# Cross-attention with routed experts: the next pair's keys and values loaded a step and a half ahead, the first normalisation in slot 2 of its own step

## The reference

```python
# 16 heads of 16; the mask pads queries' keys, and the scores are causal
x = x + tanh(g_xattn) * (softmax(mask(heads(layernorm(x)) @ heads(ctx).T / 4)) @ heads(ctx) @ W.T + b)
z = layernorm(x)
shared = swiglu(z @ w_in.T) @ w_out.T
# 2 groups of 4 experts: argmax of the group, softmax inside it, the top 2 of it by weight w_se
routed = sum over e of (swiglu(z @ w1.T) * w_se[:, e]) @ w2[e].T
x = x + tanh(g_ffn) * (shared + routed)
```

## Time and profile before

| | us |
|---|---|
| median of 3 runs (1431.3 to 1433.97) | 1433.58 |
| the profiled execution | 1430.63 |
| its span, first to last instruction | 1428.8 |
| PE busy in the span | 1201.9 (84%) |
| DVE busy | 865.6 (61%) |
| ACT busy | 502.2 (35%) |
| POOL busy | 552.0 (39%) |

### The profile page before, as it was taken

The page is one execution under the profiler, slowest core; times in us unless marked ns, Lnnn a source line. Parts: engine busy times, 40 slices in busy tenths (PEclk is TensorE's granted clock), DMA queues, the critical chain, the costliest instruction groups (busy, mean ns, idle before and its releaser), DMA issues.

```text
span 1428.8 us, 22394 instructions
## 1 busy us (share of the span) xinstructions
PE 1201.9 (84%) x7387; PEld 953.1 (67%) x7387; DVE 865.6 (61%) x1968; ACT 502.2 (35%) x780; POOL 552.0 (39%) x658
## 2 busy tenths in 40 slices
PE   0577988888888888888888898626999999999997
PEld 0245766666666666666766666525888888888886
DVE  4435667466466567566466567773666666666665
ACT  3334434443444444444443443222222222222221
POOL 1112222422422422422522514354555656555543
PEclk9989999999999899999899899867999999999999
DMA  5466435445435335435435321343222222222210
GB/s 161 85 112 114 93 81 100 85 83 95 88 74 100 84 80 101 85 80 100 86 80 98 73 47 46 75 118 83 63 71 65 65 68 73 65 64 66 69 42 9
DMA packets 108263, 115.30 MB, mean 81 GB/s; under 512 B 36942, under 2 KB 88433, under 8 KB 108148
## 3 DMA queue, kind: packets, MB, share of 16 engines
q1 hardware_dynamic: 96376, 85.41, 29.1%
q0 software_dynamic: 11776, 28.46, 6.7%
HBM read 50.44 MB, written 28.64 MB: 55 GB/s over the span
## 4 chain that ended last, share of the span: by engine, by line
PE 57%; DVE 10%; DMA 8%; POOL 8%; issue 7%; SPq 5%; ACT 4%; POOLq 0%; ACTq 0%; DVEq 0%
PE ps L681 14%; PE ps L699 10%; DMA af<-in_ctxT 7%; PE ps L702 5%; PE ps L635 5%; PE ps L618 5%; POOL tab_dram L1375 3%; PE ps L541 3%; PE ps L526 3%; PE ps L550 3%; POOL gl L1358 2%; SPq L421 2%; PE ps L502 2%; PE ps L497 2%; PE ps L594 1%
## 5 line engine op out<-in xcount | busy, mean ns | idle before, releaser
L699 PE MATMUL ps<-w2a,gh 128*128 x608 | 218.7, 399 | 0.0
L702 PE MATMUL ps<-w2a,gl 128*128 x608 | 170.6, 281 | 0.0
L759 ACT ACTIVATE Pt<-ps,pbias 77x1024 f32<-77x1024 f32 x128 | 141.5, 1106 | 73.6 <-PE ps L528 73.1
L1358 POOL TENSOR_TENSOR gl<-gf,gh 128x512 fp32r<-128x512 f32 x64 | 82.6, 1290 | 148.1 <-ACT gh L801 148.1
L1303 POOL TENSOR_SCALAR ve<-mv 128x2 f32<-128x2 f32 x64 | 15.6, 244 | 317.0 <-DVE mv L882 316.4
L1411 POOL DMA_INDIRECT out<-ot,Pt x76 | 78.4, 1032 | 153.2 <-DVE ot L1232 149.7
L699 PEld LDWEIGHTS ps<-w2a,gh 128*128 128x128 f32 x608 | 114.3, 188 | 25.2
L681 PE MATMUL ps<-z2h,w1h 128*128 128x512 f32 x304 | 122.0, 401 | 7.4 <-DVE z2l L886 7.4
L618 PE MATMUL ps<-x2h,winh 128*128 128x512 f32 x256 | 124.3, 486 | 2.4 <-DVE gf L1157 1.5
L1093 DVE TENSOR_REDUCE mneg<-ps 128x8 f32<-128x616 f32 x128 | 101.6, 795 | 35.8 <-PE ps L502 35.7
L681 PE MATMUL ps<-z2l,w1h 128*128 128x512 f32 x304 | 121.1, 398 | 0.0
(11 more groups left out here) (205 smaller groups left out, 2858.7 us busy)
## 6 DMA issues: line engine op xcount, KB each, us to landing
w2a<-w2a SPq DMA_DIRECT2D x96, 256.0 KB, 5.8
af<-in_x SPq DMA_DIRECT2D x32, 256.0 KB, 4.1
x<-in_x SPq DMA_DIRECT2D x32, 256.0 KB, 7.0
y_dram<-xn SPq DMA_DIRECT2D x32, 256.0 KB, 3.5
y_dram<-res SPq DMA_DIRECT2D x32, 256.0 KB, 2.6
w2a<-w2a SPq DMA_DIRECT2D x96, 77.0 KB, 2.8
Pt<-in_w2T SPq DMA_DIRECT2D x16, 256.0 KB, 3.0
af<-in_ctxT SPq DMA_DIRECT2D x16, 154.0 KB, 6.8
```

What stands on the lines that cost most here:

```text
L699: e.matmul(o, gh2[:, c % 2, fc, t * P:(t + 1) * P], w2v[:, bass.ds(val, 1), fc, :, :].rearrange("p o h d -> p (o h) d"), start=fc == 0, st ...
L702: m = e.matmul(o[:, 0, :], gl2[:, c % 2, fc, t * P:(t + 1) * P], w2v[:, bass.ds(val, 1), fc, 0, :].rearrange("p o d -> p (o d)"), start=Fa ...
L759: e.activation(Pt[0:K, 4 * k:4 * k + 4, :].rearrange("k (n j) t -> k n (j t)", n=2), bank_of["sc", b, k][0:K, :, :], ACT.Exp, bias=pbias[: ...
L1358: e.tensor_tensor(gl[:, fc - 1, :], gf[:, n % 2, :], gh[:, fc - 1, :].bitcast(F), ALU.subtract).then_inc(s["gl"], 1)
```

## The change

Three things move in `phase_one`; no stage is added, taken away or changed inside.

- kv moves from slot 0 to slot 3 of the even step, and load_kv of the next pair from the end of the odd step to slot 8 of the even step, so that it stands 19 slots before the kv that reads it.
- norm of batch i moves from slot 11 of step i-1 to slot 2 of step i. The norm of batch 0, which stood ahead of the steps, is in slot 2 of step 0.
- load_x of batch i+2 moves from slot 0 of step i to slot 3, behind kv, since it has to follow the norm that frees the buffer.

```diff
     order += [("load_x", 0, 0), ("load_x", 1, 0), ("load_kv", 0, 0), ("own", 0, 0), ("moments", 0, 0),
-              ("norm", 0, 0), ("masks", 0, 0)]
+              ("masks", 0, 0)]
...
-        put(i, ((7, "xT", 0), (10, "queries", 0)))
-        put(i + 1, ((8, "moments", 0), (11, "norm", 0)))
+        put(i, ((2, "norm", 0), (7, "xT", 0), (10, "queries", 0)))
+        put(i + 1, ((8, "moments", 0),))
         if i % 2 == 0 and i < NB:
-            slots[0].append(("kv", i // 2, 0))
+            slots[3].append(("kv", i // 2, 0))
+            if i + 2 < NB:
+                slots[8].append(("load_kv", i // 2 + 1, 0))
...
-            if slot == 0 and i + 2 < NB:
+            if slot == 3 and i + 2 < NB:
                 order.append(("load_x", i + 2, 0))
...
-        if i % 2 == 1 and i < NB - 1:
-            order.append(("load_kv", i // 2 + 1, 0))
```

## The result

| | before | after |
|---|---|---|
| median of 4 runs each, us | 1432.44 | 1341.51 (1338.39 to 1343.35) |
| profiled execution | 1430.63 | 1338.39 |
| its span | 1428.8 | 1336.6 |
| mean granted clock | 0.929 | 0.953 |

The ratio is 0.9373, 95% interval 0.9335 to 0.941: faster, by 91 us of the medians and 92.2 us of the two profiled spans.

The account below looks back on a forecast made before the run. TensorE was the engine to fill, stalled behind the key load. Gains 4.9 + 3.4 + 14.5 + 6 x 2.7 + 6 x 4.0 = 63 us off 1430.63 gave 1367.6, forecast as 1369; main range 1355 to 1385, 8-in-10 range 1336 to 1404.

Parts of the forecast that it names:

- The load's stall: TensorE's waits at L550 behind the key load: 59.2 us of gaps, plus up to 33 us lost at the lower clock.
- The start and the pairs without routing: Before the routed pairs: 4.9 us from the weights' splits, 3.4 in the first pair, 14.5 in the other two.
- What is late next in B: POOL's fixed chain from scatters to gl sets the limit; TensorE waits longer than 3.34 us at L635; gain about 3.2 us.
- B: Six pairs of steps whose eight routing scatters run on POOL in the first step; forecast gain 4.0 us each (2.6 to 5.5).
- The norm: First normalisation moved to slot 2: 4.9 us at the start, 0.88 us at gl in each B, nothing in A.
- A: Six pairs of steps with routing arithmetic on DVE in both steps; forecast gain 2.7 us each (1.0 to 4.4).
- The two gaps: TensorE waits left in A: 1.2 us at O, about 1.75 at the max matmul; 1.7 us of low clock charged for both.
- Rival 1: Nothing takes the place of TensorE's stalls: 64 + 33 + 4.9 = 102 us gained, so 1331 us; chance 0.15 (1331 to 1355).
- Rivals 3 and 4: maxT's DMA late in SyncE's queue: either no gain left, 1433 us, chance 0.05, or slower, 1459 us, chance 0.04.
- I take 0: Loss from maxT's DMA L424 landing later behind the moved loads: taken as 0 us, at most 39 us in 15 pairs.
- The other signs: Phase one's mean clock above 0.91, ACT's and POOL's waits for the load gone, weights' split on ACT 4.9 us earlier.

Follow-up runs that it names:

- the filled stall: The kernel before, with 30 unused small matmuls in front of O in each even step from the fourth on: 1410.82 us, ratio 0.9865.
- part 1 alone: The kernel before with only kv moved to slot 3 and load_kv to slot 8, norm and load_x as before: 1363.75 us, ratio 0.9507.
- part 2 alone: The kernel before with only the norm moved to slot 2 of its own step and load_x to slot 3: 1418.13 us, ratio 0.9892.
- the fastest version: The changed kernel with three routing pieces per two slots instead of four, and the second normalisation's root moved behind gl: 1274.61 us, ratio 0.8919.

## Why the prediction was right or wrong, step by step

- **The load's stall goes, and it cost twice.** Right. L550's 59.2 us are 4.9, and the filled stall shows the second cost by itself: 19 us.
- **The start and the pairs without routing.** Right: 9.3 against 8.3 (4.8 with part 1 alone and 4.8 with part 2 alone), 14.9 against 14.5. The weights' splits on ACT start at 24.99 instead of 29.49, 4.5 us earlier.
- **What is late next in B.** The place was right, POOL's fixed chain, and so was its length; that PE would wait longer there was not. PE of before, at the gl ahead of the one shown in the earlier trace rows, then PE and POOL of the changed kernel:

```profile
373.03 0.38 PE L635 MATMUL ps<-woh,gh 128*128 128x256 f32 x1 [0.69 <-POOL gl L1358]
```

```profile
408.12 1.03 PE L550 MATMUL ps<-ident,af 128*128 128x128 f32 x8
...
425.50 0.44 PE L502 MATMUL ps<-first,identb 128*128 128x308 bf16 x2 [0.48 <-POOL first L1344]
426.71 0.39 PE L635 MATMUL ps<-woh,gh 128*128 128x256 f32 x1 [0.77 <-POOL gl L1358]
...
430.78 0.58 PE L635 MATMUL ps<-woh,gh 128*128 128x256 f32 x1 [2.49 <-POOL gl L1358]
```

```profile
412.02 1.13 POOL L1375 DMA_INDIRECT tab_dram<-rec,slot  x1 [5.41 <-DVE rec L1042]
413.16 0.63 POOL L1329 COPY af<-af 77x512 f32<-77x512 f32 x1
...
425.11 0.34 POOL L1344 TENSOR_TENSOR first<-pad,caus 128x77 bf16<-128x77 bf16 x1
425.38 1.27 POOL L1358 TENSOR_TENSOR gl<-gf,gh 128x512 fp32r<-128x512 f32 x1
...
428.77 0.72 POOL L1305 TENSOR_TENSOR rs<-ve,mhalf 128x2 f32<-128x2 f32 x1
429.44 1.28 POOL L1358 TENSOR_TENSOR gl<-gf,gh 128x512 fp32r<-128x512 f32 x1
```

  O does not wait; from O to the first scatter are 3.9 us (4.1 forecast); the kv copy stands behind that scatter and costs nothing that shows; gl is not held by gh any more. From the first scatter to the end of gl are 18.7 us, 19.8 in before (358.12 to 377.88), of which the forecast took off 0.88. But the wait at L635 is 2.49 us, not "longer than the 3.34 us": PE meets POOL's lateness already at `first` (0.48, where it did not wait before) and at the gl ahead (0.77, 0.69 before), so it is paid in three pieces, 3.7 us in sum against 4.0.
- **The norm.** It was worth more than the 4.9 + 6 x 0.88 = 10 us forecast: some 15 alone, 19 on top of part 1. "0.88 us" was right as a length (0.86 in part 2 alone). Leaving its clock out was wrong: with it the low time behind the waits at gl falls from 9.6 to 7.4 us per cycle (A and B together), and PE's busy time by another 1.2.
- **In A: the step that failed.** "Each may cost up to 1.7 us ... I take 1.7 for both together: A gains 2.7". The two gaps are there, but smaller, and cost hardly any clock. PE in A, then windows behind these two gaps, and last behind B's gl:

```profile
458.40 1.06 PE L550 MATMUL ps<-ident,af 128*128 128x128 f32 x8 [0.62 <-ACT Pt L759]
467.10 0.41 PE L497 MATMUL ps<-w2a 64*128 64x308 f32 x2 [1.24 <-DVE mneg L1093]
```

```profile
458.40:463.00 4.60, 4.60 (x31) 3.74 (x32) 3.21 (x10) 3.55 (x6) 0.00 (x0) 1.00 0.39 98
467.10:471.00 3.90, 3.90 (x17) 3.25 (x18) 2.96 (x11) 0.60 (x1) 0.00 (x0) 0.56 0.36 124
430.80:436.90 6.10, 6.10 (x27) 5.47 (x28) 3.06 (x7) 0.00 (x0) 1.55 (x2) 0.50 0.45 140
```

  O waits 0.62 us (1.2 forecast), the max matmul 1.24 (1.75 forecast). The window at 467.10 is the only low one behind such a gap in the six A: 0.6 us at the lower level per cycle, 0.3 us lost, where the forecast charged 1.7. (The last row, B's gl, is where most of the low clock is left.)
- **The size of the miss.** Put together from its own terms, the forecast's 6.7 us per cycle were 5.4 of idle time (A: 3.5 less 0.85; B: 3.12 less 1.2 plus 0.88) and 1.3 of clock (A: 1.6 less 1.7; B: 1.4). Measured: 10.9, 6.7 of idle time and 4.3 of clock. So of the 4.2 us missed per cycle 3.0 are clock and 1.2 are gaps that came out smaller; six cycles make 25 of the 29 us. The clock term was mis-sized at both ends. Behind the stalls at O PE was busy at the lower level for 66.01 / 14 = 4.7 us each, so the two of a cycle give 4.7 back, of which I credited 1.6 + 1.4 and, against that, charged 1.7 for gaps that cost 0.3. Half of the changes at the two gl (2.3 to 1.7 in A, 4.5 to 5.7 in B) is -0.3: 4.7 - 0.3 - 0.3 = 4.1, near the 4.3 measured. That 1341.5 still lies inside the 8-in-10 range is owed to the width of that range, not to this sum.
- **Rival 1 came closest**, yet its "nothing takes the stalls' place" is not quite what happened: 54 us of stalls at O went and idle time fell by 49.8, so some of it came back at other waits. 68 us of idle time are left, of which the fastest version has 27. Rival 1 is near in time since it gave the whole clock behind the stalls back (33 us; 31.9 measured).
- **Rivals 3 and 4, the queue.** "I take 0" for L424 holds for A and nearly for B: PE's waits for maxT's DMA were 15.1 us in 6 waits, against 8.3 in 4. "No PE wait for w2a<-w2a in slot 1" was wrong at 101.52 (5.36 us, 1.34 in before) and in two B; the three other waits stand in before as well. That the trace had no landing for L424 was a misreading: the chain has 3.26 us, 0.9 less than the 4.12 at hand, and in the new place it has 4.89 and 6.18 where PE waited for it. The rule of the Trainium skill cited in the prediction (DMA: Bandwidth & Descriptors, Queues, rings and completion order) ties an increment to the earlier writes of its own SDMA engine. The trace agrees in that the landing took longest right behind the loads, 4.89 and 6.18 us; no run here separates order in the ring from transfers that only run side by side.
- **The other signs.** Phase one's mean clock is 0.96 (above 0.91), ACT's and POOL's waits for the load are gone, and the load lands 2.84 us after its issue at 95.44 (98.28), where load_x and the kv DMAs, and no queries, are issued ahead of it.

Still open: what decides whether a wait at L635 lowers the clock (the last section).

## What to carry to other kernels

A load that a busy engine waits for in order can be worth more than its wait: price the stall, then the busy time behind it at the lower clock, and check that second part by filling the stall with idle matmuls. When several gaps go at once, don't charge the ones that stay with a low clock that other gaps brought; bound it from none to all, and take the whole low stretch behind each gap that goes. After the first wait is gone, look at what stands in front of the late instruction on its own queue (here a root ahead of gl, and the density of the routing pieces): those two moves brought 67 us more here.

## What was not expected of the hardware

The lower clock does not follow from the length of one gap. In the changed kernel alone the same wait at A's gl was followed by the full clock in three of six A and by a low stretch in three. PE, then windows of five microseconds right behind:

```profile
191.62 0.38 PE L635 MATMUL ps<-woh,gh 128*128 128x256 f32 x1 [1.79 <-POOL gl L1358]
...
674.68 0.39 PE L635 MATMUL ps<-woh,gh 128*128 128x256 f32 x1 [1.83 <-POOL gl L1358]
```

```profile
675.00:680.00 5.00, 5.00 (x30) 4.53 (x29) 3.68 (x11) 0.35 (x2) 1.57 (x2) 0.66 0.92 222
193.00:198.00 5.00, 5.00 (x43) 4.67 (x42) 4.62 (x12) 1.71 (x2) 1.56 (x2) 1.00 0.74 196
```

1.79 us and then 1.00; 1.83 us and then 0.66. And issuing a DMA on SyncE took 2.25 us at 323.70 and 2.05 us at 615.82, where the same instructions mostly take 0.47 and 0.38 us; both put maxT's DMA behind. Scatters of POOL's ran beside both, but they are not shown to be the cause: one also ran beside the issue at 325.99, which took 0.38, and in before six issues at L414 took 4.71 us at 410.32, against 3.87, with no scatter beside them. SyncE, then the PE wait that followed:

```profile
323.70 2.25 SPq L393 DMA_DIRECT2D af<-in_ctxT  x1
...
326.42 0.68 SPq L424 DMA_DIRECT2D w2a<-w2a  x1
...
332.85 0.68 PE L526 MATMUL ps<-w2a 100*77 100x256 f32 x2 [1.91 <-DMA w2a<-w2a]
```
